# Attention block: the turned row maxima are stored by ACT's DMA queue instead of SP's

## What is computed

```python
# x (16,100,512), ctx (16,361,512); 16 query heads, 4 key heads, head size 32
xn = layernorm(x)
Q = (xn @ Wq) / sqrt(32);  K = ctx @ Wk;  V = ctx @ Wv
scores = einsum('bqghd,bkgd->bghqk', Q, K) + slope * (k - q)   # masked
w = softmax(scores);  attn = (w @ V) @ Wo
x = x + tanh(g_xattn) * attn
# feed-forward: 8 bit activations, ternary weights, silu gate, rms norm
x = x + tanh(g_ffn) * down(rms_norm(silu(gate(q8(ln(x)))) * up(q8(ln(x)))))
```

## Time and profile before

| what | us |
|---|---|
| median of 3 runs | 571.62 |
| lowest and highest run | 571.01, 575.53 |
| run with the profile | 567.73 |
| span of the profiled execution | 565.9 |
| TensorE busy in the span | 494.0 (87%) |
| VectorE busy | 364.4 (64%) |
| ScalarE busy | 345.5 (61%) |
| GpSimd busy | 221.1 (39%) |

### The profile page before, as it was taken

The page is one execution under the profiler, slowest core; times in us unless marked ns, Lnnn a source line. Parts: engine busy times, 40 slices in busy tenths (PEclk is TensorE's granted clock), DMA queues, the critical chain, the costliest instruction groups (busy, mean ns, idle before and its releaser), DMA issues.

```text
span 565.9 us, 8809 instructions
## 1 busy us (share of the span) xinstructions
PE 494.0 (87%) x3106; PEld 312.9 (55%) x3106; DVE 364.4 (64%) x671; ACT 345.5 (61%) x578; POOL 221.1 (39%) x238
## 2 busy tenths in 40 slices
PE   2799599878975999999999998579999999999984
PEld 1799599878932444444444453335555555555442
DVE  3884365257652879887887754267767766766751
ACT  2345666456543666667666766566777777777762
POOL 1010000000035876763475700265555555566540
PEclk9999899999997999999999999799999999999997
DMA  7879977999159778976687501001110001111000
GB/s 190 238 245 331 356 260 224 294 303 316 48 127 262 204 166 198 189 169 159 137 194 167 140 23 72 1 0 38 38 36 24 27 25 37 37 39 38 28 20 28
DMA packets 29259, 76.81 MB, mean 136 GB/s; under 512 B 4350, under 2 KB 15822, under 8 KB 27302
## 3 DMA queue, kind: packets, MB, share of 16 engines
q1 hardware_dynamic: 24038, 51.16, 34.3%
q0 software_dynamic: 3456, 12.58, 8.6%
q10 hardware_dynamic: 1728, 12.58, 6.5%
HBM read 57.29 MB, written 9.85 MB: 119 GB/s over the span
## 4 chain that ended last, share of the span: by engine, by line
PE 57%; DVE 11%; ACT 10%; DMA 9%; issue 7%; POOL 3%; SPq 2%; ACTq 0%; POOLq 0%; DVEq 0%
PE bank L1092 10%; PE wide L1260 9%; PE wide L1092 7%; PE bank L1185 6%; PE bank L1175 6%; PE wide L1161 6%; DMA ct<-ctx_t 5%; PE bank L1188 5%; PE bank L1280 3%; PE bank L1133 3%; DVE row_max L895 3%; ACT p_t L641 3%; ACT yq L761 2%; DMA qs<-nm_t 2%; DMA wq_f<-wq 1%
## 5 line engine op out<-in xcount | busy, mean ns | idle before, releaser
L895 DVE TENSOR_REDUCE row_max<-wide 100x2 f32<-100x722 f32 x128 | 110.2, 902 | 40.6 <-PE wide L1161 40.4
L641 ACT ACTIVATE p_t<-bank 121x400 f32<-121x400 f32 x192 | 92.3, 504 | 56.5 <-PE bank L1175 53.0
L1260 PE MATMUL wide<-w_q,xq 128*128 128x512 bf16 (+1 forms) x416 | 96.2, 380 | 0.8 <-ACT xq L688 0.8
L516 POOL TENSOR_TENSOR z<-h,lnw 128x512 f32<-128x512 f32 (+1 forms) x52 | 66.5, 1281 | 30.4 <-DVE h L1005 30.0
L736 ACT ACTIVATE act<-wide,small 128x512 f32<-128x512 f32 (+1 forms) x52 | 35.6, 687 | 49.7 <-PE wide L1260 40.5
L1260 PEld LDWEIGHTS wide<-w_q,xq 128*128 128x128 bf16 (+1 forms) x416 | 39.2, 99 | 47.7 <-issue 4.5
L475 POOL DMA_DIRECT2D quant_in<-w_ffn x24 | 14.3, 595 | 125.1 <-DVE small L886 118.6
L1175 PE MATMUL bank<-qs,ks 103*121 103x400 f32 x144 | 50.5, 382 | 11.3 <-DMA qs<-nm_t 8.1
L1161 PE MATMUL wide<-ks,qs 101*100 101x362 f32 x192 | 49.5, 345 | 8.2 <-DVE row_max L895 5.6
L1280 PE MATMUL bank<-w_q,yq 128*128 128x512 bf16 (+1 forms) x208 | 50.9, 391 | 1.9 <-ACT yq L761 0.8
L1133 PE MATMUL bank<-wv_f,ct 128*121 128x128 f32 x384 | 45.1, 274 | 4.6 <-DMA ct<-ctx_t 4.6
(11 more groups left out here) (137 smaller groups left out, 929.0 us busy)
## 6 DMA issues: line engine op xcount, KB each, us to landing
quant_in<-w_ffn POOLq DMA_DIRECT2D x24, 512.0 KB, 6.5
ct<-ctx_t SPq DMA_DIRECT2D x16, 722.0 KB, 9.4
abs_b<-w_ffn ACTq DMA_DIRECT2D x8, 1024.0 KB, 9.8
ks<-k_all SPq DMA_DIRECT2D x36, 181.0 KB
q_scratch<-qhl SPq DMA_DIRECT2D x16, 400.0 KB, 5.6
qs<-q_scratch SPq DMA_DIRECT2D x12, 400.0 KB
abs_a<-w_ffn ACTq DMA_DIRECT2D x4, 1024.0 KB, 7.8
xb<-x SPq DMA_DIRECT2D x12, 256.0 KB, 2.6
```

The lines of the kernel that those rows point to most:

```text
L516: nc.gpsimd.tensor_tensor(z[par][0:rows, c], h[0:rows, c], lnw[0:rows, c], ALU.mult).then_inc(z_done, 1)
L641: nc.scalar.activation(p_t[:, j, :], bank[j % 2][0:KT, 0:HQ], ACT.Exp).then_inc(exp_done, 1)
L895: nc.vector.tensor_reduce(row_max[b % 2][:, 2 * u:2 * u + 2], wide[u % 2][0:SQ, :, 0:SK], AX_X, ALU.max).then_inc(s_maxed, 1)
L1260: mm = nc.tensor.matmul(wide[j % 2][0:rows, m, :], xq[:, c, 0:rows], w_q[:, m * C + c, 512 * j:512 * j + 512], start=(c == 0), stop=(c == ...
```

## The change

The function store_max moves from SP's program into ACT's, and with it the wait for nm_ready and the two dma_start. ACT calls it right behind each turned_max: for batches 1 to 15 in its attention step, for batch 0 in the context loop at b == 12. SP's step keeps the loads alone, and its loop ends after step 14, since steps 15 and 16 held only the store.

```diff
-            def store_max(b):
-
-                sp.wait_ge(nm_ready, b + 1)
-                for part in range(2):
-                    sp.dma_start(qs[b % SLOTS][ROWS_S + part:ROWS_S + part + 1, :, :].bitcast(F32).rearrange("p g (h q) -> p (g h) q", h=HPG),
-                                 nm_t[H * part:H * part + H, :].bitcast(F32)).then_inc(nm_in, 16)
-
             def attention_step(b):
-                store_max(b - 1)
                 if b == 1:
...
-            for b in range(1, B + 1):
+            for b in range(1, B - 1):
                 attention_step(b)
...
+            def store_max(b):
+
+                act.wait_ge(nm_ready, b + 1)
+                for part in range(2):
+                    act.dma_start(qs[b % SLOTS][ROWS_S + part:ROWS_S + part + 1, :, :].bitcast(F32).rearrange("p g (h q) -> p (g h) q", h=HPG),
+                                  nm_t[H * part:H * part + H, :].bitcast(F32)).then_inc(nm_in, 16)
+
...
                 if 2 <= b <= B:
                     turned_max(b - 1)
+                    store_max(b - 1)
...
                 if b == 12:
                     turned_max(0)
+                    store_max(0)
```

## The result

| | before | changed |
|---|---|---|
| median, us | 571.32 (4 runs) | 591.92 (4 runs) |
| ratio to before, 95% interval | | 1.0392 (1.0338 to 1.0447) |
| span of the profiled execution | 565.9 | 590.1 |
| mean granted clock of TensorE, share of 2.4 GHz | 0.976 | 0.953 |

What follows compares the result with a forecast made beforehand. TensorE's own work, broken in each batch by an exponential on ACT, was taken as the bound, plus one 8.1 us stall. 17.8 us of delay less 7.4 gained gives +10.4, median 582.0 us, range 573.5 to 587.5.

Steps and rivals of the forecast that it cites:

- The price of an issue and who waits behind it: On ACT behind the copy: each issue takes 0.586 us, exponentials start 1.37 us late, TensorE's eleventh product 1.36 us late.
- The rival of cheap issues: ACT needs only 0.334 us per issue, a step costs 0.87 us, span 575.5 us; chance 0.15.
- the absorbed delay: Rival: the 1.37 us vanish in ACT's 1.67 us idle time, only the gain remains, 564.2 us; chance 0.11.
- How many steps: Attention loop: steps 3 to 15 pay in full, 13 x 1.37 = 17.8 us; step 16 and batch 0's store cost nothing.
- The 0.08 us to spare for batch 0: Context loop: the delayed split ends at 142.85 us, DVE takes the block up at 142.93, so zero cost.
- So a step costs 1.37 us: Steady attention step: the delay on ACT passes to TensorE in full, 1.37 us, with nothing absorbed by ACT's idle time.
- The gain of step 2: Batch 1's store no longer waits behind load_qk(3); the stall goes and batch 3's scores start 7.4 us earlier (5.9 to 8.2).
- lands 2.6 us later: Step 2: batch 1's store, second issue at 162.99 us, lands at 165.6 us, before TensorE asks at 168.21.
- the next limit: Step 2: batch 3's scores next wait for load_qk(3), landing between 171.8 and 174.9 us, middle 173.4.
- The rival of the stall that stays: Step 2: the store lands only after the engines work off the loads, the gain is lost, 589.4 us; chance 0.08.
- The shared descriptor generator: Step 2: ACT's issues could take longer while SP issues, 1.2 us more in one step, 0.9 of it hidden.

Runs made afterwards that it cites:

- experiment 3: The kernel before, with ACT waiting for its own copy of the maxima but issuing no DMA; 573.43 us against 573.98, ratio 1.0015.
- experiment 5: The changed kernel, with one DMA issue on ACT for both parts of the maxima instead of two; 584.03 us against 571.16 for the kernel before, ratio 1.020.
- experiment 6: The changed kernel, with a third DMA issue of the same size per batch on ACT; 607.08 us, ratio 1.063 to the kernel before.
- experiment 4: The changed kernel, with five unread matmuls in TensorE's gap in each of steps 3 to 15; 587.12 us against 573.98 for the kernel before, ratio 1.026.
- experiment 1: The kernel before, with only the store of batch 1 moved to ACT; 573.76 us against 573.98, ratio 0.998.
- experiment 9: The kernel before, with GpSimd's first two loads behind the store of batch 1 and the stores of batches 1 and 2 on ACT; 570.57 us against 573.24.
- experiment 8: The kernel before, with GpSimd's first two weight loads waiting until the maxima of batch 1 are stored; 566.35 us against 571.16, ratio 0.989.
- experiment 10: The kernel before with GpSimd's first two loads behind the store of batch 1, measured again in more rounds; 567.71 us against 573.24, ratio 0.990.

## Why the prediction was right in direction and wrong in size

*The price of an issue and who waits behind it.* Right. A median of 0.566 to 0.603 us was measured on ACT for the 0.586 taken from SP's rows, 1.31 us a step for 1.37. The rival of cheap issues (0.334 us) falls, and so does the absorbed delay: ACT's idle time of 1.67 us is there after the change too, and absorbed nothing. Experiments 3, 5 and 6 show the cost by issue.

*How many steps.* Right where TensorE's time alone is counted: 13 x 1.31 = 17.0 us for 17.8, and nothing for the store of batch 0 or in step 16 (the product behind the output projection starts 2.92 us behind the copy in both kernels). The 0.08 us to spare for batch 0 were not there, though: a load of w_ffn is issued on ACT at the same place, the split began 2.2 us behind the copy's start instead of the 1.6 forecast, and VectorE waited 1.4 us for it. TensorE's products there run without a gap.

*The step that failed: "So a step costs 1.37 us".* The delay was priced as a pure shift. It is an idle time of 1.1 us on TensorE in each batch, and in 4 of 13 steps the clock fell behind it, 7.1 us in all. Why in these four steps and not in the others, no run shows. The earlier trace rows had the same thing for the 8 us stall, and the prediction took note of it there, as a gain, but did not ask what a new gap on the same engine does. This is the term that was missing; experiment 4 takes the low clock away and gives 7.4 us back. With it the sum is 17.8 + 7.1 - 7.4 = 17.5 us, a median of 589.1 us. The range, to 587.5, had no room for it.

*The gain of step 2.* 7.4 us forecast, 5.9 in the profiled execution, 3.7 in that of experiment 4. Two terms of it failed. "lands 2.6 us later" was 7.4 us; the middle of all landings was the wrong row, since it is one of steps with less traffic, and the row beside it with the DMA share of 1.04 was the nearer. And TensorE asked for the store 7.6 us behind the copy, not 6.1, because the gap of 1.1 us let its clock fall there too:

```profile
171.00:172.00 1.00, 1.00 (x8) 0.22 (x7) 0.50 (x1) 0.43 (x1) 0.92 (x2) 0.50 1.05 265
```

So the missing term took about 1.5 us here as well, and hid most of the late landing: only 0.6 us of waiting were left. The loads of batch 3, which the prediction took for the next limit, were not waited for. The rival of the stall that stays had the mechanism half right: the landing was nearly as late as before (9.4 us in experiment 1, 9.5 in experiment 5), but the issue came sooner, and TensorE later. The chance of 0.08 was too low for it. The rule of the Trainium skill that was cited for it (DMA: Bandwidth & Descriptors, Issuing engines are not separate DMA queues) is borne out: on a queue of its own the store took 9.4 us instead of 9.2 (experiment 1), and 4.7 instead of 4.4 and 4.6 with GpSimd's loads away (experiments 9, 8 and 10). What that page adds, that issue time is usually small beside the transfer, is not so here: two issues take 1.2 us and the transfer lands in 2.6, and it is the issue that costs.

*The shared descriptor generator.* In step 2 ACT issued its pair from 166.53 to 167.70 while SP was issuing until 167.46, and took 1.17 us as in other steps. No lengthening in this run. In experiment 1 the pair took 1.40 us while SP was issuing as well, 0.2 us more than usual.

*What adds up to 20.6.* 24.2 us in the loop, less 5.9, is 18.3 us; with the 3.7 of experiment 4 it is 20.5. The 2.3 us between 18.3 and the 20.6 of the medians are within what step 2 and the stretches before and after the loop scatter by, and are not divided further.

## What to carry to other kernels

An engine whose busy share is 61% can still be the tight one at one place: before a DMA issue is put on a computing engine, look at what stands right behind it there, and whether another engine has any slack against that. A gap of one microsecond that is cut into TensorE in each iteration has two prices, its length and the clock that may fall behind it; a gap of half the length, or harmless work in the gap, kept the second at nothing here. And a small transfer that lands late beside large ones was helped by issuing it ahead of them or by keeping them away for these microseconds, not by another queue; whether the time gains depends on what the moved loads hold up in turn.

## What was not expected of the hardware

Matmuls that nobody reads, put into TensorE's idle time, took 7.4 us out of 177. An idle time of 1.1 us a step let the clock fall in some steps of the same program and not in others (4 of 13 in the one profiled execution), while one of 0.6 us (one issue) did it in none of 13; ahead of the loop three idle times of 0.57, 0.41 and 0.19 us in a row did it in some executions. And a 12 KB store, alone on its queue, needed 9.4 us to land while two other queues kept the engines full, against 2.6 us on SP just ahead of one group of these loads, and 1.7 us at best.
